# Three-layer graph network: the first two edge steps of layers 1 and 2 gathered before the last two node chunks are stored

## The chip, the core and the metric

One of the eight cores of a Trainium2 chip runs the whole program. The metric is device time in microseconds (us) for one execution, as the median of several. Its engines are named as in the profile: PE (TensorE), DVE (VectorE), ACT (ScalarE), POOL (GpSimd) and SP (SyncE, which only issues DMAs here). "SPq" and "ACTq" are DMAs being issued by SP and ACT.

## What is computed

The reference encodes 12,500 nodes of 64 features, runs three message-passing layers over 212,500 edges sorted by destination, and ends with a readout, a residual and a layer norm. Cut to what matters:

```python
h = node_features @ enc_W + enc_b
for l in range(N_LAYERS):
    cat = jnp.concatenate([h[src], h[dst], edge_features], axis=-1)
    m = jax.nn.relu(cat @ msg_W1[l] + msg_b1[l]) @ msg_W2[l] + msg_b2[l]
    agg = jax.ops.segment_sum(m, dst, num_segments=n_nodes)
    h = _gru_cell(agg, h, gru_Wih[l], gru_Whh[l], gru_bih[l], gru_bhh[l])
return jax.nn.relu(h @ ro_W1 + ro_b1) @ ro_W2 + ro_b2
```

An edge reads its source's row of `h`, so a layer's edges can read any node: layer l + 1 needs every row that layer l makes.

## The kernel before, in words

**Tables.** The product of `h` with the source part and with the destination part of `msg_W1` is made once per node, at the end of a layer's node work, and stored in HBM: `p_tab[l]` (sources) and `q_tab[l]` (destinations), 64 floats a row. An edge then needs a row of `p_tab` (a gather by `src`), a row of `q_tab` (sorted, so a window of 48 rows read by a plain DMA and spread with a one-hot product) and its own attributes.

**Steps.** The edges of a layer are cut into 208 steps of 1,024 edges (8 tiles of 128; the last step has 5). For every step:
- POOL issues one indirect DMA per tile (L734), 128 rows of 256 bytes each, into one of 7 slots of `p_src`. In every fourth step (3, 7, 11, ...) the eighth tile is left to SP and ACT, which issue 64 DMAs of one row each (`single_rows`, L441), so POOL issues 7.
- PE makes the edge part (L872) and the destination part (L873) in PSUM (`mix`). DVE adds the edge part to the gathered rows (L1410, `edge_sums`), adds the destination part (L1413, this sets `joined`), applies relu and a mask (L1424, `drop_masked`), folds runs (L1429, `fold`), and PE spreads the folded rows to nodes (L885). DVE adds these to `sums` (L1439, `keep`, sets `kept`).
- POOL may fill a slot again once the step seven before has been joined.

**Chunks.** The nodes are cut into 26 chunks of 468, then one of 144 and one of 192 (`SPANS`, 28 in all). When the steps that reach a chunk are kept, its GRU runs in stages put between the steps (`chunk_stages`, `fast_chunk`): ACT copies its sums (L1072, L1073), PE makes the gates (L929, L930), ACT and DVE the nonlinear part, PE the next layer's two table rows (L937), ACT copies them to `stage` (L1083) and issues the two stores (L1086, L1087), which raise `stored[0]`. The chunk with index 25 is stored while steps 205 and 206 run, index 26 while step 207 runs, and index 27 after step 207, the last (`END_STAGES`).

**The boundary between layers.** `all_stored` makes POOL, SP and ACT wait until all 28 chunks' tables are in HBM. Then SP and ACT load the windows of the first two groups of four steps (L603, L1111), POOL starts the gathers of step 0, and SP starts the single rows of step 3. The order on each engine is written out by hand, unrolled over layers and steps; only semaphores order the engines among each other:

```python
for l in range(LAYERS):
    all_stored(pool, l, FAST_CHUNKS)
    for m in range(STEPS):
        k, r = l * STEPS + m, (l * STEPS + m) % ROW_SLOTS
        if k >= ROW_SLOTS:
            pool.wait_ge(joined, k - ROW_SLOTS + 1)
        for t in range(gathers_of(m)):
```

## Time and profile before

| | |
|---|---|
| median of 3 runs | 6212.81 us (6212.6 to 6212.83) |
| the profiled execution's own time | 6218.49 us |
| its span, first to last instruction | 6216.6 us |
| POOL busy | 4625.3 us (74%), of it L734 4599.4 us in 4830 instructions |
| DVE busy | 3524.2 us (57%) |
| PE busy | 2874.1 us (46%), weight loads 1569.7 us |
| ACT busy | 345.5 us (6%) |
| DMA | 307.50 MB, mean 49 GB/s |
| chain that ended last | POOL 69%, issue 23%, SPq 3%, DVE 2%, DMA 2%, PE 1% |

How to read it: busy time counts compute and the indirect DMAs' descriptor work on POOL; DMA issues of SP and ACT, waits and register work do not count. The last row follows the work that ended last back to what released each piece of it; "issue" is time in which the engine waited for nothing that the profile shows, here the 0.3 us between two indirect DMAs.

### The profile page before, as it was taken

To read this page: it belongs to the slowest core of one execution; us is meant where nothing else is said; L and a number is where in the kernel's file an instruction comes from. 1 tells how busy PE (TensorE), PEld (TensorE's weight loads), DVE (VectorE), ACT (ScalarE), POOL (GpSimd) and SP (SyncE) were. 2 spreads that over 40 slices of the span, in tenths; PEclk is the share of its full clock that TensorE was granted. 3 is DMA by queue.
4 is the path that set the end of the run, shared out by engine and by line. 5 is a ranking of instruction groups with operands and counts; after the bars stand their busy time and mean duration, and the time that the engine had idled before them with its cause. 6 is when DMAs were issued, how large, how long until landed. Compare 5 with 4: busy or idle time off the path is not lost.

```text
span 6216.6 us, 71434 instructions
## 1 busy us (share of the span) xinstructions
PE 2874.1 (46%) x6986; PEld 1569.7 (25%) x6986; DVE 3524.2 (57%) x4596; ACT 345.5 (6%) x542; POOL 4625.3 (74%) x4865
## 2 busy tenths in 40 slices
PE   4444444444444444444444444444444444444444
PEld 3222222222222222222222222222222222222222
DVE  5555555555555555555555555555555555555555
ACT  1000000000000000000000000000000000000001
POOL 6777777777777677777777777767777777777776
PEclk6666666666656655656555565556566565656656
DMA  4222222222222122222222222212222222222221
GB/s 127 50 49 49 49 49 49 49 49 49 49 49 49 40 48 48 48 48 48 47 48 48 48 48 48 48 44 47 48 48 47 46 49 45 48 48 48 48 48 36
DMA packets 350333, 307.50 MB, mean 49 GB/s; under 512 B 148483, under 2 KB 236553, under 8 KB 349463
## 3 DMA queue, kind: packets, MB, share of 16 engines
q0 software_dynamic: 155328, 159.81, 13.6%
q1 hardware_dynamic: 117167, 109.08, 6.1%
q10 hardware_dynamic: 77328, 33.96, 2.1%
q14 instruction: 453, 3.71, 0.2%
q8 instruction: 57, 0.93, 0.1%
HBM read 279.43 MB, written 22.83 MB: 49 GB/s over the span
## 4 chain that ended last, share of the span: by engine, by line
POOL 69%; issue 23%; SPq 3%; DVE 2%; DMA 2%; PE 1%; ACT 0%; DVEq 0%; ACTq 0%; POOLq 0%
POOL p_src L734 69%; SPq L441 2%; SPq L437 1%; DMA q_tab<-p_src 1%; DVE work_ps L1413 1%; DMA p_src<-p_tab,idx_all 0%; DMA p_src<-p_tab 0%; DVE p_src L1410 0%; PE bank L929 0%; PE bank L930 0%; DVE folds L1429 0%; PE bank L765 0%; DVE state L1448 0%; ACT p_src L994 0%; PE bank L885 0%
## 5 line engine op out<-in xcount | busy, mean ns | idle before, releaser
L734 POOL DMA_INDIRECT p_src<-p_tab,idx_all x4830 | 4599.4, 952 | 1559.0 <-issue 1471.1
L1410 DVE TENSOR_TENSOR p_src<-work_ps,p_src 128x512 f32<-128x512 f32 x624 | 431.2, 691 | 2495.6 <-DMA p_src<-p_tab,idx_all 2283.5
L885 PE MATMUL bank<-hot,folds 128*128 128x96 f32 x2496 | 657.1, 411 | 1855.2 <-DVE folds L1429 1787.9
L872 PE MATMUL work_ps<-w_edges,msg 128*128 128x512 f32 x1248 | 1115.9, 994 | 28.3 <-DMA windows_sb<-q_tab 28.3
L885 PEld LDWEIGHTS bank<-hot,folds 128*128 128x128 f32 x2496 | 528.3, 294 | 2124.6 <-DVE folds L1429 1996.6
L1424 DVE SCALAR_TENSOR_TENSOR work_ps<-work_ps,rel 128x1024 f32<-128x1024 f32 x624 | 768.5, 1232 | 21.5
L1413 DVE TENSOR_TENSOR work_ps<-p_src,bank 128x1024 f32<-128x1024 f32 x624 | 766.8, 1229 | 21.2
L1429 DVE TENSOR_REDUCE folds<-work_ps 128x256 f32<-128x1024 f32 x624 | 757.6, 1214 | 0.1
L882 PE MATMUL bank<-hot,counts 128*34 128x96 bf16 x416 | 66.9, 254 | 909.7 <-DVE folds L1429 909.7
L929 PE MATMUL bank<-state,gate_w 128*128 128x468 f32 x324 | 266.8, 923 | 454.5 <-ACT chunk_sum L1073 324.5
L872 PEld LDWEIGHTS work_ps<-w_edges,msg 128*128 128x128 f32 x1248 | 309.5, 303 | 29.6 <-issue 15.8
L873 PE MATMUL bank<-pick 97*128 97x256 f32 x624 | 313.4, 604 | 0.0
L882 PEld LDWEIGHTS bank<-hot,counts 128*34 128x34 bf16 x416 | 26.6, 106 | 1027.0 <-DVE folds L1429 1006.1
L873 PEld LDWEIGHTS bank<-pick 97*128 97x128 f32 x624 | 204.9, 328 | 312.4 <-issue 312.4
L873 PE MATMUL bank<-windows_sb,pick 97*128 97x256 f32 x624 | 281.0, 546 | 0.0
L873 PEld LDWEIGHTS bank<-windows_sb,pick 97*128 97x128 f32 x624 | 181.1, 290 | 265.2 <-issue 265.2
L929 PEld LDWEIGHTS bank<-state,gate_w 128*128 128x128 f32 x324 | 93.2, 319 | 589.7 <-issue 428.6
L930 PE MATMUL bank<-chunk_sum,sum_w 128*128 128x468 f32 x324 | 225.5, 791 | 0.0
L1072 ACT COPY chunk_sum<-sums 64x468 f32<-64x468 f32 (+1 forms) x84 | 47.3, 563 | 3123.2 <-DVE sums L1439 3118.2
L1439 DVE TENSOR_TENSOR sums<-bank,sums 128x96 f32 x624 | 156.5, 251 | 5.6 <-PE bank L885 2.7
L1383 DVE TENSOR_TENSOR hot<-rel_first,bank 128x784 f32<-128x784 f32 x156 | 149.7, 959 | 0.0
L930 PEld LDWEIGHTS bank<-chunk_sum,sum_w 128*128 128x128 f32 x324 | 96.5, 300 | 123.2 <-issue 123.2
(157 smaller groups left out, 1428.1 us busy)
## 6 DMA issues: line engine op xcount, KB each, us to landing
p_src<-p_tab ACTq DMA_DIRECT2D x9792, 0.2 KB
p_src<-p_tab SPq DMA_DIRECT2D x9792, 0.2 KB
p_src<-p_tab,idx_all POOLq DMA_INDIRECT x4830
msg<-in_edge_k SPq DMA_DIRECT2D x156, 256.0 KB
pick<-rel_tab SPq DMA_DIRECT2D x312, 96.0 KB
windows_sb<-q_tab ACTq DMA_DIRECT2D x312, 24.0 KB
windows_sb<-q_tab SPq DMA_DIRECT2D x312, 24.0 KB
pick<-q_tab ACTq DMA_DIRECT2D x312, 24.0 KB
```

What stands on the lines that cost most here:

```text
L734: pool.indirect_dma_start(out=p_src[r][0:rows, t, :], out_offset=None, in_=p_tab[l][0:NODES, :], in_offset=bass.IndirectOffsetOnAxis(ap=id ...
L872: nc.tensor.matmul(edge_ps[k % 2], attrs[n % 2][:, s, :], w1_edges[:, l, :], start=True, stop=True)
L873: nc.tensor.matmul(node_ps[k % 2], hot_rows[n % 2][0:ROWS + 1, s * 128:(s + 1) * 128], windows_of[k % (2 * GROUP)][0:ROWS + 1, :], start=T ...
L885: last = nc.tensor.matmul(fold_ps, folds[:, b, :], hot_all[n % 2][:, s * BLOCKS + b, 1:WINDOW + 1], start=(b == 0), stop=(b == BLOCKS - 1))
L929: nc.tensor.matmul(ps[:, 0:w], gate_w[:, l, g:g + 128], state[:, here], start=True, stop=False)
L930: end = nc.tensor.matmul(ps[:, 0:w], sum_w[:, l, g:g + 128], chunk_sum[:, 0:w], start=False, stop=True)
L1383: nc.vector.tensor_tensor(hot_all[n % 2][:], first, spots_ps.unsqueeze(1).to_broadcast([128, GROUP * BLOCKS, HOT]), ALU.is_equal)
L1410: nc.vector.tensor_tensor(rows, edge_ps[k % 2], rows, ALU.add).then_inc(with_edge, 1)
L1413: nc.vector.tensor_tensor(both_ps[k % 2].rearrange("p (f b j g) -> p b j g f", b=BLOCKS, j=2, g=RUN), rows.rearrange("p (b g f) -> p b g f ...
L1424: nc.vector.scalar_tensor_tensor(runs, runs, 0.0, edge_masks, ALU.max, ALU.mult).then_inc(masked, 1)
L1429: nc.vector.tensor_reduce(folds[:].rearrange("p b (j f) -> p (b j) f", j=2), both_ps[k % 2].rearrange("p (f e g) -> p e f g", g=RUN, f=HID ...
L1439: nc.vector.tensor_tensor(sums[:, here], fold_ps, sums[:, here], ALU.add).then_inc(kept, 1)
```

## The change

Two constants say what is early: `EARLY = 2` steps of layers 1 and 2, and `LATE = 26 * 468 = 12168`, the first node of the last two chunks. The "late" rows are the 336 from 12168 to 12504, in three blocks of 112.

- **POOL**, in layers 1 and 2, first waits only for the first 26 chunks' stores and for two cleared slots. It gathers steps 0 and 1 from `p_tab[l][0:LATE]` with a bounds check that skips a row beyond it (`oob_is_err=False`). Only ahead of step 2 does it wait for all stores.
- **DVE** clears those two slots at step 204 of the layer before (two memsets of 128 x 512).
- **SP** loads the late rows of `p_tab` into SBUF (one DMA of 112 x 3 x 64) between the window loads of groups 0 and 1 of layers 1 and 2. In layer 0 it also loads the sources of steps 0 and 1, repeated over 112 partitions (two DMAs of 112 x 1024).
- **DVE** compares these sources with the late nodes' numbers (`make_late`): 12 one-hot tiles of 112 x 256 for each early step, in a ring of four buffers. Each tile after the fourth waits for PE.
- **PE** multiplies them by the late rows (24 matmuls of 112 x 128 by 112 x 64 for each early step) into a PSUM bank, ahead of that step's `mix`.
- **DVE** adds the bank to the slot (`add_late`, one 128 x 512 add) ahead of `edge_sums`.
- Four tiles of the final layer norm become slices of one (`normed`) that also holds the one-hot ring. Three small DVE operations at the start make the late nodes' numbers.

```diff
+            if l:
+                pool.wait_ge(stored[0], 32 * (FAST_CHUNKS * (l - 1) + CHUNKS - 1 + ENC_PAIRS // 2))
+                pool.wait_ge(slots_clear, EARLY * l)
             for m in range(STEPS):
                 k, r = l * STEPS + m, (l * STEPS + m) % ROW_SLOTS
                 if k >= ROW_SLOTS:
                     pool.wait_ge(joined, k - ROW_SLOTS + 1)
+                if early(l, m):
+                    for t in range(gathers_of(m)):
+                        pool.indirect_dma_start(
+                            out=p_src[r][:, t, :], out_offset=None, in_=p_tab[l][0:LATE, :],
+                            in_offset=bass.IndirectOffsetOnAxis(ap=idx_all[:, m, t:t + 1], axis=0),
+                            bounds_check=LATE - 1, oob_is_err=False).then_inc(gathered[r], 16)
+                    continue
+                if m == (EARLY if l else 0):
+                    all_stored(pool, l, FAST_CHUNKS)
...
                         group_windows(l, n0 + g, g)
...
+                        if l and g == 0:
+                            sp.dma_start(late_rows, p_tab[l][LATE:NLAST, :].rearrange("(b p) f -> p b f", p=LATE_ROWS)).then_inc(late_in, 16)
+                    if l == 0:
+                        sp.wait_ge(prepared, 8)
+                        for m in range(EARLY):
+                            sp.dma_start(src_seen[m], io["src_early"][m:m + 1, :].to_broadcast([LATE_ROWS, STEP])).then_inc(early_in, 16)
...
+                if early(l, m):
+                    pe.wait_ge(late_in, 16 * l)
+                    for q in range(4):
+                        hots = nth_late(l, m, q, 0)
+                        pe.wait_ge(late_ready, hots + LATE_BLOCKS)
+                        for t in range(2):
+                            at = (2 * q + t) * HID
+                            for b in range(LATE_BLOCKS):
+                                last = nc.tensor.matmul(late_ps[m][:, at:at + HID], late_hot[(hots + b) % 4][:, t * 128:(t + 1) * 128], late_rows[:, b, :],
+                                                        start=(b == 0), stop=(b == LATE_BLOCKS - 1))
+                        last.then_inc(late_mixed, LATE_BLOCKS)
...
+            def make_late(l, m):
+                for q in range(4):
+                    for b in range(LATE_BLOCKS):
+                        i = nth_late(l, m, q, b)
+                        if i >= 4:
+                            dve.wait_ge(late_mixed, (i - 4) // LATE_BLOCKS * LATE_BLOCKS + LATE_BLOCKS)
+                        nc.vector.tensor_tensor(late_hot[i % 4], src_seen[m][:, q * QUARTER:(q + 1) * QUARTER], late_node[:, b:b + 1].to_broadcast([LATE_ROWS, QUARTER]),
+                                                ALU.is_equal).then_inc(late_ready, 1)
+            def add_late(l, m):
+                k = l * STEPS + m
+                rows = p_src[k % ROW_SLOTS].rearrange("p t f -> p (t f)")
+                dve.wait_ge(gathered[k % ROW_SLOTS], landed(k))
+                dve.wait_ge(late_mixed, nth_late(l, m, 0, 0) + LATE_HOTS)
+                nc.vector.tensor_tensor(rows, late_ps[m], rows, ALU.add).then_inc(late_added, 1)
+                dve.wait_ge(late_added, (l - 1) * EARLY + m + 1)
...
+                        if l and m == 0:
+                            dve.wait_ge(early_in, 16 * EARLY)
+                            make_late(l, 0)
+                        if early(l, m):
+                            add_late(l, m)
                         edge_sums(k)
                         drop_masked(k)
+                        if early(l, m + 1):
+                            make_late(l, m + 1)
+                        if m == STEPS - 4 and l < LAYERS - 1:
+                            for j in range(EARLY):
+                                nc.vector.memset(p_src[(k + 4 + j) % ROW_SLOTS], 0.0).then_inc(slots_clear, 1)
```

The order of instructions, engine by engine, shows where these land. POOL's whole gather order, in the kernel before:

```order
L724 COMPARE_AND_BRANCH
L734 DMA p_src<-p_tab,idx_all 128x64 x1609
L734 DMA p_src<-p_tab,idx_all 20x64
L734 DMA p_src<-p_tab,idx_all 128x64 x1609
L734 DMA p_src<-p_tab,idx_all 20x64
L734 DMA p_src<-p_tab,idx_all 128x64 x1609
L734 DMA p_src<-p_tab,idx_all 20x64
L724 UNCONDITIONAL_BRANCH
```

And in the changed one:

```order
L755 COMPARE_AND_BRANCH
L776 DMA p_src<-p_tab,idx_all 128x64 x1609
L776 DMA p_src<-p_tab,idx_all 20x64
L767 DMA p_src<-p_tab,idx_all 128x64 x16
L776 DMA p_src<-p_tab,idx_all 128x64 x1593
L776 DMA p_src<-p_tab,idx_all 20x64
L767 DMA p_src<-p_tab,idx_all 128x64 x16
L776 DMA p_src<-p_tab,idx_all 128x64 x1593
L776 DMA p_src<-p_tab,idx_all 20x64
L755 UNCONDITIONAL_BRANCH
```

The count and order of gathers is the same; 16 in each of layers 1 and 2 (L767) have moved ahead of the wait for all stores, which now stands between them and the 1593.

PE at the start of layer 1, from the last chunk's table product (`w_nodes`) on, in the kernel before:

```order
L937 MATMUL bank<-w_nodes,state 96x128 x2
L872 MATMUL work_ps<-w_edges,msg 128x512
L873 MATMUL bank<-windows_sb,pick 128x256
L872 MATMUL work_ps<-w_edges,msg 128x512
L873 MATMUL bank<-windows_sb,pick 128x256
L885 MATMUL bank<-hot,folds 128x96 x2
```

And in the changed one, where `dst_i` is the memory that holds the late rows and `normed` the one-hot ring:

```order
L990 MATMUL bank<-w_nodes,state 96x128 x2
L922 MATMUL bank<-dst_i,normed 128x64 x24
L925 MATMUL work_ps<-w_edges,msg 128x512
L926 MATMUL bank<-windows_sb,pick 128x256
L922 MATMUL bank<-dst_i,normed 128x64 x24
L925 MATMUL work_ps<-w_edges,msg 128x512
L926 MATMUL bank<-windows_sb,pick 128x256
L938 MATMUL bank<-hot,folds 128x96 x2
```

Each of the first two steps' products now stands behind 24 small ones, and the second 24 stand ahead of the first step's spreading (L938).

DVE at the same place, from the last chunk's new state on, in the changed kernel (before, L1464 is followed at once by L1410, L1413, L1424, L1429 of step 0):

```order
L1536 TENSOR_TENSOR state<-bank,zdiff 64x192
L1478 TENSOR_TENSOR normed<-dst_i,late_node 112x256 x12
L1487 TENSOR_TENSOR p_src<-bank,p_src 128x512
L1463 TENSOR_TENSOR p_src<-work_ps,p_src 128x512
L1466 TENSOR_TENSOR work_ps<-p_src,bank 128x16x64
L1496 SCALAR_TENSOR_TENSOR work_ps<-work_ps,rel 128x1024
L1478 TENSOR_TENSOR normed<-pre,late_node 112x256 x12
L1501 TENSOR_REDUCE folds<-work_ps 128x256
L520 TENSOR_LOAD base_i
L1487 TENSOR_TENSOR p_src<-bank,p_src 128x512
L1463 TENSOR_TENSOR p_src<-work_ps,p_src 128x512
L1466 TENSOR_TENSOR work_ps<-p_src,bank 128x16x64
```

The second step's twelve one-hot tiles stand between the first step's mask (L1496) and its fold (L1501).

## Rows read from the trace of the kernel before

**Rows 1.** The page's busy times, and what its engines waited for: POOL.
```profile
PE 2874.1 (46%) x6986; PEld 1569.7 (25%) x6986; DVE 3524.2 (57%) x4596; ACT 345.5 (6%) x542; POOL 4625.3 (74%) x4865
POOL p_src L734 <- issue: 1471.1, 4817, 0.3
POOL p_src L734 <- DMA q_tab<-stage: 47.2, 2, 27.9
POOL p_src L734 <- DMA q_tab<-p_src: 37.7, 1, 37.7
```
**Rows 2.** Timeline of POOL between layers 0 and 1 (start, us, engine, line, [idle before]).
```profile
2088.18 0.92 POOL L734 DMA_INDIRECT p_src<-p_tab,idx_all  x1 [0.30 <-issue]
2116.98 0.98 POOL L734 DMA_INDIRECT p_src<-p_tab,idx_all  x1 [27.89 <-DMA q_tab<-stage]
...
2137.13 0.95 POOL L734 DMA_INDIRECT p_src<-p_tab,idx_all  x1 [0.31 <-issue]
```
**Rows 3.** The same between layers 1 and 2.
```profile
4140.43 0.90 POOL L734 DMA_INDIRECT p_src<-p_tab,idx_all  x1 [0.30 <-issue]
4160.66 0.98 POOL L734 DMA_INDIRECT p_src<-p_tab,idx_all  x1 [19.33 <-DMA q_tab<-stage]
```
**Rows 4.** Timeline between layers 0 and 1, the other engines: last stores, first step.
```profile
2085.27 0.40 ACTq L1087 DMA_DIRECT2D q_tab<-stage  x1
2114.76 0.44 ACTq L1087 DMA_DIRECT2D q_tab<-stage  x1
2121.49 2.05 PE L872 MATMUL work_ps<-w_edges,msg 128*128 128x512 f32 x2 [7.53 <-DMA windows_sb<-q_tab]
2122.47 24.93 SPq L441 DMA_DIRECT2D p_src<-p_tab  x64
2123.33 1.06 PE L873 MATMUL bank<-windows_sb,pick 97*128 97x256 f32 x2
2128.77 0.69 DVE L1410 TENSOR_TENSOR p_src<-work_ps,p_src 128x512 f32<-128x512 f32 x1 [16.02 <-DMA p_src<-p_tab,idx_all]
2129.49 1.23 DVE L1413 TENSOR_TENSOR work_ps<-p_src,bank 128x1024 f32<-128x1024 f32 x1
```
**Rows 5.** Timeline between layers 1 and 2, around steps 204 and 206.
```profile
4119.58 0.25 DVE L1439 TENSOR_TENSOR sums<-bank,sums 128x96 f32 x1
4119.86 0.58 ACT L1072 COPY chunk_sum<-sums 64x468 f32<-64x468 f32 x1 [17.37 <-DVE sums L1439]
4136.83 0.69 DVE L1410 TENSOR_TENSOR p_src<-work_ps,p_src 128x512 f32<-128x512 f32 x1 [0.16 <-DMA p_src<-p_tab,idx_all]
```
**Rows 6.** Groups by form (busy us, mean ns of one): nearest to the added operations.
```profile
L1499 DVE MEMSET pick<- 128x512 f32 x2 | 1.0, 485 | 0.1
L1478 DVE TENSOR_TENSOR ysq<-yc 117x256 f32<-117x256 f32 x26 | 11.0, 425 | 0.9
L1505 DVE TENSOR_TENSOR rel_first<-dst_i,base_all 128x416 f32<-128x416 int32 x1 | 0.8, 754 | 0.0
L781 PE MATMUL bank<-w_nodes,enc_b_last 64*97 64x64 f32 x4 | 0.9, 380 | 1.1 <-ACT count_w L1002 1.1
```
**Rows 7.** Timeline: spreading matmuls, first at the lower and then at the higher clock.
```profile
2133.30 1.17 PE L885 MATMUL bank<-hot,folds 128*128 128x96 f32 x4 [7.37 <-DVE folds L1429]
2053.54 0.69 PE L885 MATMUL bank<-hot,folds 128*128 128x96 f32 x4
```
**Rows 8.** Timeline in layer 2: gathers beside a DVE operation with two SBUF inputs.
```profile
6150.32 0.95 POOL L734 DMA_INDIRECT p_src<-p_tab,idx_all  x1 [0.30 <-issue]
6150.55 0.42 DVE L1478 TENSOR_TENSOR ysq<-yc 117x256 f32<-117x256 f32 x1
6151.58 0.95 POOL L734 DMA_INDIRECT p_src<-p_tab,idx_all  x1 [0.30 <-issue]
```
**Rows 9.** What SP's queue waited for (us in total, times, longest).
```profile
SPq L591 <- PE bank L873: 906.5, 103, 35.7
SPq L610 <- DVE sums L1439: 400.8, 28, 17.0
```

More of the change, by code:

```diff
@@ L54 @@
 GATHER_SLOTS = LOOP_STEPS
+EARLY = 2
+LATE = (CHUNKS - 1) * CHUNK
+LATE_BLOCKS = 3
+LATE_ROWS = (NLAST - LATE) // LATE_BLOCKS
+QUARTER = STEP // 4
+LATE_HOTS = 4 * LATE_BLOCKS
 LAST_EDGES = EDGES - (STEPS - 1) * STEP
@@ L135, in build @@
         masks = rel[:].rearrange("p s t -> p (s t)").bitcast(BF16).rearrange("p (b j g) -> p b j g", j=2, g=RUN)
+        dst_flat = dst_i[0:LATE_ROWS].rearrange("p s t -> p (s t)")
+        late_rows = dst_flat[:, STEP:STEP + LATE_BLOCKS * HID].bitcast(F32).rearrange("p (b f) -> p b f", f=HID)
+        late_node = sb("late_node", [LATE_ROWS, LATE_BLOCKS])
         rel_first = sb("rel_first", [128, STEPS, BLOCKS])
@@ L179, in build @@
         offsets = p_src[ROW_SLOTS].rearrange("p t f -> p (t f)")[0:GROUPS, 0:128].bitcast(I32)
+        src_seen = [dst_flat[:, 0:STEP], both[0:LATE_ROWS, :].bitcast(I32)]
         first_i = both[0:STEPS // 2, 0:2 * BLOCKS * 128].bitcast(I32)
@@ L202, in build @@
         x_rows = sb("x_rows", [CPART, 4, HID])
-        y = sb("y", [CPART, 4, HID])
-        yc = sb("yc", [CPART, 4, HID])
-        ysq = sb("ysq", [CPART, 4, HID])
+        normed = sb("normed", [CPART, 4, 4, HID])
+        y, yc, ysq, y_out = (normed[:, s] for s in range(4))
+        late_hot = [normed[0:LATE_ROWS, s].rearrange("p j f -> p (j f)") for s in range(4)]
         ysum = sb("ysum", [CPART, 4])
@@ L211, in build @@
         rstd = sb("rstd", [CPART, 4])
-        y_out = sb("y_out", [CPART, 4, HID])
         bank = [ctx.enter_context(nc.psum_tensor(f"bank{i}", [128, 512], F32)) for i in range(5)]
@@ L292, in build @@
         act_singles = [sem(f"act_singles{s}") for s in range(SINGLE_SEMS)]
+        early_in = sem("early_in")
+        slots_clear = sem("slots_clear")
+        late_in = sem("late_in")
+        late_ready = sem("late_ready")
+        late_mixed = sem("late_mixed")
+        late_added = sem("late_added")
         hot_t_ready = sem("hot_t_ready")
@@ L419, in run_slow, with early, nth_late @@
                     chunk_stage(l, j, LOOPED, last)
+        def early(l, m):
+            return l > 0 and m < EARLY
+        def nth_late(l, m, q, b):
+            return ((l - 1) * EARLY + m) * LATE_HOTS + q * LATE_BLOCKS + b
+        late_ps = [zr_ps[:], n_ps[:]]
         def gathers_of(m):
@@ L726, in _ @@
                 for l in range(LAYERS):
-                    all_stored(pool, l, FAST_CHUNKS)
+                    if l:
+                        pool.wait_ge(stored[0], 32 * (FAST_CHUNKS * (l - 1) + CHUNKS - 1 + ENC_PAIRS // 2))
+                        pool.wait_ge(slots_clear, EARLY * l)
                     for m in range(STEPS):
@@ L1508, in _ @@
                 nc.vector.tensor_copy(row_ps, row_f[:]).then_inc(in_psum, 1)
-                dve.wait_ge(in_psum, 2)
+                for b in range(LATE_BLOCKS):
+                    nc.vector.tensor_scalar(late_node[:, b:b + 1], row_i[0:LATE_ROWS, :], 1.0, float(LATE + LATE_ROWS * b), ALU.mult, ALU.add).then_inc(in_psum, 1)
+                dve.wait_ge(in_psum, 2 + LATE_BLOCKS)
                 make_hot(0)
@@ L1588 @@
         "src_single": src[GROUP - 1::GROUP, BLOCKS - 1, :, RUN - 1],
+        "src_early": src[0:EARLY].transpose(0, 1, 3, 2).reshape(EARLY, STEP),
         "dst": dst[place].transpose(2, 0, 1, 3).reshape(128, STEPS, EDGE_TILES),
@@ L1612 @@
         arrays[name] = v = np.ascontiguousarray(v)
-        dt = U32 if name == "src" else I32 if name.startswith("dst") or name == "src_single" else F32
+        dt = U32 if name == "src" else I32 if name.startswith("dst") or name.startswith("src_") else F32
         if name == "src":
```

## The prediction

> **What bounds the kernel now.** I read the busy times and POOL's waits first. POOL is busy for 74% of the span, DVE for 57%, PE for 46% [rows 1]. POOL's idle time is nearly all accounted for in three rows: 1471.1 us in 4817 gaps of at most 0.3 us between two gathers, which is part of issuing one, 37.7 us before the first gather, and 47.2 us in two waits for `q_tab` stores. So POOL never pauses inside a layer. One gather takes 0.95 + 0.30 us; over the 16 from 2116.98 to 2137.13 that is 1.26 us each [rows 2]. 4830 of them, with the three waits and the tail, are the kernel. DVE and PE are waited for only at the layers' ends.
>
> Next, the timeline at both boundaries. Between layers 0 and 1 the last gather starts at 2088.18 and the next at 2116.98: 27.89 us idle [rows 2]. Between layers 1 and 2 it is 19.33 us [rows 3]. In both, what ends the wait is the last chunk's `q_tab` store, issued at 2114.76 and landed when POOL starts 2.22 us later [rows 2, 4]. Call that moment T, the time at which all tables are stored. Only POOL's idle time ahead of T can be won, so the most that this change can give is 27.9 + 19.3 = 47.2 us, less what early work doesn't fill.
>
> **The change, part by part.**
>
> *The 16 moved gathers.* 16 at 1.26 us are 20.15 us. At the first boundary POOL would go on at 2089.4, end its 16 at 2109.6, and wait 7.4 us for T at 2116.98. Step 2 then starts at 2117.0 in place of 2137.13: 20.1 us won, if T stays. At the second, the next gather would have started near 4141.6; 16 later is 4161.75, after T (4160.66). Before, step 2 started 16 gathers after 4160.66, at 4180.8. That is 19.0 us won, with POOL never idle.
>
> *May they start that early?* They wait for chunk 25's stores. At the first boundary its `q_tab` store is issued at 2085.27 [rows 4]; with the 2.22 us that the last store took, it has landed at 2087.5, 1.9 us ahead of POOL's need. The slots are cleared and joined some twenty us earlier.
>
> *The two memsets at step 204*, 128 x 512 each: 0.485 us by the like form [rows 6], with gaps 1.0 us of DVE ahead of the `keep` that releases chunk 25. At the first boundary DVE soon after stands 0.95 us idle for PE, so I take 0.1 us (0 to 1.0). At the second, `keep` at 4119.58 releases ACT at 4119.86 directly, and DVE follows with hardly a gap until step 206, which stood 0.16 us for its gather [rows 5]: T moves by 1.0 - 0.16 = 0.84 us, to 4161.5. POOL arrives at 4161.75 anyway, so it costs nothing there (bounds 0 and 0.8 us, if POOL comes first).
>
> *The skipping bounds check* has no row. Every gather here is of the plain kind, at 1.26 us [rows 2]. Below: nothing, since the skipped rows (336 of 12504 nodes, 3 or 4 of 128 rows) might even save packets, but POOL's own part is fixed. Above I have only DVE's row for an operation with an extra input, which says nothing of POOL; I bound it by another 0.95 us, doing a gather's work twice. I take nothing, as 125 of the 128 rows take the plain path. The first boundary hides 7.4 us, that is 0.46 us a gather; the second hides none.
>
> *The late rows' products.* They lie behind T, on PE and DVE, and POOL feels them only through a slot: step 8 refills step 1's. After T POOL issues the gathers of steps 2 to 7, 46 of them (8 + 7 + 8 + 8 + 8 + 7), which is 57.9 us. So step 1 must be joined by T + 57.9.
> - Start: PE began step 0 at 2121.49, T + 4.5 [rows 4]; one more SP DMA stands between the windows, so T + 5.
> - A matmul: 112 x 128 weights and 64 columns. The nearest row is L781, 97 columns of weights and 64 moving, 0.91 us for two (four passes), 0.46 each; the other side is L885, 128 weights and 96 moving, 1.17 us for two, 0.59 each [rows 6, 7]. I take 0.5, so 3.0 us for the six of a quarter (2.7 to 3.5 at the lower clock; 2.1 at the higher, by the 0.69 us row).
> - A one-hot tile: 112 x 256 with two SBUF inputs, by L1478 0.425 us plus a gap, 0.46; above, L1505's int32 form at 0.754 [rows 6].
> - The ring of four holds one tile more than a quarter. So after the first quarter DVE makes two tiles while PE waits, then PE runs six matmuls while DVE waits: 0.9 + 3.0 + 0.3 for the hand-overs = 4.2 us a round. A step is 3.0 + 3 x 4.2 = 15.6 us.
> - Step 0: products until T + 20.6, edge and destination parts (2121.49 to 2124.39) 2.9, the two adds 2.0 [rows 4]: joined at T + 25.5. The mask 1.3, three tiles 1.4, products 15.6, parts 2.9, adds 2.0: step 1 joined at T + 48.7.
>
> That is 9 us ahead of POOL's need, so I put the products at zero. With 3.5 us and 0.754 us a round is 5.4 us and step 1 is joined at T + 57.8, still free. Behind it DVE needs some 5.5 us a step and POOL 9.7, so the lag of DVE is gone by about step 7, and step 9 (POOL at T + 68) needs step 2, at about T + 56.
>
> *SP.* Its single rows of step 3 took 24.93 us [rows 4] and end near T + 34, before DVE comes to step 3. Group 2's inputs wait for `mixed` of step 3, now near T + 55, then step 7's 64 rows end near T + 85. POOL needs step 7 joined for step 14, at T + 117. SP stood idle 906.5 us for PE in 103 waits [rows 9], so it catches up within a few groups.
>
> *Start and end.* In layer 0 two more DMAs and three tiny DVE operations stand ahead of nothing that POOL waits for; the final chain only changes the addresses of four tiles. Nothing.
>
> **Sum.** 20.1 - 0.1 + 19.0 = 39.0 us. Against the profiled execution: 6218.5 - 39.0 = 6179.5. That execution stands 5.7 us above the median of the runs; against the median, 6212.8 - 39.0 = **6173.8 us**, 0.63% faster. About 0.2%, 12.4 us, is what a measurement of this kernel can tell from no change.
>
> **A rule weighed.** Twelve of a step's tiles have two SBUF inputs and run while POOL gathers. In layer 2 such an operation (0.42 us at 6150.55) lies across two gathers of 0.95 us that start 1.26 us apart [rows 8], the same as everywhere; it cost POOL nothing. The Trainium skill, page "SBUF — State Buffer", section "SBUF: two separate sides", says that DVE and GpSimd share a port pair, taken for a whole instruction by a DVE operation with two SBUF inputs against a GpSimd operation that reads SBUF, and that the other is blocked. The trace does not agree for these gathers; the rule's time is the third rival.
>
> **Rivals.**
> 1. *The products come too late, and a new wait on `joined` replaces the old one.* For it: DVE and PE take turns, nothing like this ring has a row, and waits add up over six rounds. Against it: 9 us of room. It costs from 5.7 us a round on. At 9 us it eats the whole gain (six rounds by 4.8 more are 28.8, less 9.1 of room, 19.7 a boundary). At 11 us a round, 6.8 more in each of six, the stall is 31.7 us a boundary, and the kernel is slower by 63.4 - 39.0 = 24.4 us: 6237. A milder form, 8 us a round, stalls 13.7 a boundary: 6201.
> 2. *The skipping gathers cost more.* Nothing speaks for it but the missing row. At 0.95 us more a gather the 16 take 15.2 us more: 15.2 - 7.4 = 7.8 at the first boundary and 15.2 at the second, so 23 of 39 us are lost: 6197.
> 3. *The one-hot tiles hold POOL back.* If each of the 48 delays a gather by its own 0.425 us, that is 20.4 us: 6194. Against it, rows 8.
> 4. *It doesn't start early.* Chunk 25's stores land later beside the extra traffic, or a slot is not free, and POOL waits about as long as before: the 1.9 us of margin at the first boundary is thin, though beyond it a delay costs only its own length. All of the gain lost: 6213.
>
> **Chances.** The forecast 0.83; the products 0.03 in the strong form and 0.02 in the mild; the gathers 0.05; the tiles 0.03; not early 0.04. Faster by over 0.2% (below 6200.4): forecast, gathers and tiles, 0.91. Within 0.2%: the mild products and not early, with some of what else could be wrong, 0.06. Slower: 0.03. The forecast's own range is 6171 to 6182: from 2 us under the sum (39.5 us with no memset cost, and a like shift of the program's other parts) to both memsets counted in full and stores that land a few us later beside POOL's gathers. I reach to 6190 for a price of the skip of up to half a us and for part of rival 3: **6171 to 6190**.
>
> **What would show it.** POOL's idle before the first early gather 0.3 us at both boundaries; before step 2, about 7.5 us and 0.3 us; the early gathers 0.95 us each; no POOL wait on L1466 (`joined`) behind it; step 1's L1466 done by T + 49, with PE and DVE taking turns every 4.2 us. Wrong: early gathers longer than 1.4 us, a POOL wait at step 7, 8 or 9, or T more than 1 us later after POOL's last gather than before.

## The result, and the profile after

| | before | changed |
|---|---|---|
| median of the runs of one chip, us | 6212.82 (6212.6 to 6213.8, 4 runs) | 6175.56 (6174.51 to 6177.06, 4 runs) |
| ratio, 95% interval | | 0.9939 [0.9926, 0.9953] |
| profiled execution, us | 6218.49 | 6174.51 |
| its span, us | 6216.6 | 6172.7 |

The forecast was 6173.8 us, in a range of 6171 to 6190. The time came 1.8 us above it; the medians differ by 37.3 us, and the forecast said 39.0. The two profiled executions differ by 43.9 us of span, more than the medians, because the one of before stands 5.7 us above its median and the one of the changed kernel 1.05 below.

First the busy times of the changed kernel's page, and what POOL waited for (us in total, times, longest us), which answer to [rows 1].

```profile
PE 2896.9 (47%) x7178; PEld 1598.8 (26%) x7178; DVE 3544.3 (57%) x4655; ACT 345.5 (6%) x542; POOL 4626.0 (75%) x4865
POOL p_src L776 <- issue: 1466.0, 4785, 5.2
POOL p_src L776 <- DMA q_tab<-p_src: 35.2, 1, 35.2
POOL p_src L767 <- issue: 9.7, 32, 0.3
POOL p_src L776 <- DVE work_ps L1466: 3.7, 12, 0.3
```

The two waits of 47.2 us for `q_tab<-stage` are gone from the list. PE does 192 matmul records more and DVE 59 operations more, and neither shows up among what POOL waits for: its longest wait for DVE's join (L1466) is 0.3 us, the ordinary gap.

Now POOL's timeline at the first boundary (start, us, engine, line, [idle before]), the answer to [rows 2].

```profile
2084.60 0.91 POOL L776 DMA_INDIRECT p_src<-p_tab,idx_all  x1 [0.31 <-issue]
2085.82 1.06 POOL L767 DMA_INDIRECT p_src<-p_tab,idx_all  x1 [0.30 <-issue]
...
2105.50 1.00 POOL L767 DMA_INDIRECT p_src<-p_tab,idx_all  x1 [0.30 <-issue]
2111.68 0.96 POOL L776 DMA_INDIRECT p_src<-p_tab,idx_all  x1 [5.18 <-issue]
```

And at the second, for [rows 3].

```profile
4115.11 0.90 POOL L776 DMA_INDIRECT p_src<-p_tab,idx_all  x1 [0.30 <-issue]
4116.32 1.05 POOL L767 DMA_INDIRECT p_src<-p_tab,idx_all  x1 [0.30 <-issue]
...
4136.13 1.00 POOL L767 DMA_INDIRECT p_src<-p_tab,idx_all  x1 [0.30 <-issue]
4137.58 0.96 POOL L776 DMA_INDIRECT p_src<-p_tab,idx_all  x1 [0.45 <-issue]
```

POOL goes from its last plain gather to the first early one without a stop, issues 16 of them 1.31 us apart, and waits 5.18 us for T at the first boundary and 0.45 at the second. (The profile puts these waits down to "issue"; they end within 0.4 us of the start of SP's windows, which wait for the same stores, at 2111.31 and 4137.18, so I read them as waits for T.)

Last, DVE and PE with POOL in between, in the first step's products, and the joins of steps 0 and 1 (L1487 adds the late rows, L1466 joins). A matmul leaves two records in these rows, so x12 is a quarter's six.

```profile
2116.16 2.79 PE L922 MATMUL bank<-dst_i,normed 112*128 112x64 f32 x12 [7.96 <-DMA windows_sb<-q_tab]
2118.99 1.09 DVE L1478 TENSOR_TENSOR normed<-dst_i,late_node 112x256 f32<-112x256 int32 x3 [10.54 <-PE bank L922]
2119.81 2.82 PE L922 MATMUL bank<-dst_i,normed 112*128 112x64 f32 x12 [0.85 <-DVE normed L1478]
2122.66 1.10 DVE L1478 TENSOR_TENSOR normed<-dst_i,late_node 112x256 f32<-112x256 int32 x3 [2.58 <-PE bank L922]
2123.06 1.19 POOL L776 DMA_INDIRECT p_src<-p_tab,idx_all  x1 [0.30 <-issue]
2123.48 2.82 PE L922 MATMUL bank<-dst_i,normed 112*128 112x64 f32 x12 [0.85 <-DVE normed L1478]
...
2133.39 1.23 DVE L1466 TENSOR_TENSOR work_ps<-p_src,bank 128x1024 f32<-128x1024 f32 x1
2150.97 0.69 DVE L1487 TENSOR_TENSOR p_src<-bank,p_src 128x512 f32<-128x512 f32 x1 [1.85 <-PE bank L922]
2154.39 1.23 DVE L1466 TENSOR_TENSOR work_ps<-p_src,bank 128x1024 f32<-128x1024 f32 x1
```

The turns of PE and DVE are plain to see: 2116.16, 2119.81, 2123.48, one every 3.67 us. Step 0 is joined at 2134.62, T + 23.3, and step 1 at 2155.62, T + 44.3 (T here is the start of SP's windows, 2111.31; counted from POOL's own start after T, 0.37 us later, they are 22.9 and 43.9). POOL issues step 8's first gather, which needs step 1's slot, at 2170.48, after the ordinary 0.30 us. And one thing that is new: the gather at 2123.06, beside three one-hot tiles, took 1.19 us where its neighbours take 0.95.

### The profile page after: what moved, and what is told of

Read it like the earlier page. It is cut to its first block, busy times and chain, and to the rows that moved or that the text cites. A ratio compares the mean times of both kernels' runs of the same rounds, so it can differ in the third digit from the quotient of the medians.

```text
span 6172.7 us, 71924 instructions
## 1 busy us (share of the span) xinstructions
PE 2896.9 (47%) x7178; PEld 1598.8 (26%) x7178; DVE 3544.3 (57%) x4655; ACT 345.5 (6%) x542; POOL 4626.0 (75%) x4865
## 3 DMA queue, kind: packets, MB, share of 16 engines
q0 software_dynamic: 155328, 159.79, 13.6%
## 4 chain that ended last, share of the span: by engine, by line
POOL 68%; issue 23%; SPq 3%; DVE 2%; PE 2%; DMA 1%; ACT 0%; ACTq 0%; DVEq 0%; POOLq 0%
POOL p_src L776 68%; SPq L466 2%; PE bank L922 1%; DVE work_ps L1466 1%; SPq L462 1%; DMA q_tab<-p_src 1%; DMA p_src<-p_tab,idx_all 0%; DVE p_src L1463 0%; DMA p_src<-p_tab 0%; DVE folds L1501 0%; PE bank L982 0%; DVE normed L1478 0%; PE bank L983 0%; PE work_ps L925 0%; ACT p_src L1047 0%
## 5 line engine op out<-in xcount | busy, mean ns | idle before, releaser
L938 PE MATMUL bank<-hot,folds 128*128 128x96 f32 x2496 | 650.1, 408 | 1792.0 <-DVE folds L1501 1757.0
L938 PEld LDWEIGHTS bank<-hot,folds 128*128 128x128 f32 x2496 | 523.0, 291 | 2057.7 <-DVE folds L1501 1965.0
L1496 DVE SCALAR_TENSOR_TENSOR work_ps<-work_ps,rel 128x1024 f32<-128x1024 f32 x624 | 768.5, 1232 | 21.6
L1466 DVE TENSOR_TENSOR work_ps<-p_src,bank 128x1024 f32<-128x1024 f32 x624 | 766.9, 1229 | 21.3
L1501 DVE TENSOR_REDUCE folds<-work_ps 128x256 f32<-128x1024 f32 x624 | 757.7, 1214 | 0.0
L925 PEld LDWEIGHTS work_ps<-w_edges,msg 128*128 128x128 f32 x1248 | 306.3, 301 | 13.6 <-DMA windows_sb<-q_tab 13.5
L935 PEld LDWEIGHTS bank<-hot,counts 128*34 128x34 bf16 x416 | 26.6, 106 | 1029.1 <-DVE folds L1501 1008.6
```

The costliest lines, as they stand in the source:

```text
L925: nc.tensor.matmul(edge_ps[k % 2], attrs[n % 2][:, s, :], w1_edges[:, l, :], start=True, stop=True)
L938: last = nc.tensor.matmul(fold_ps, folds[:, b, :], hot_all[n % 2][:, s * BLOCKS + b, 1:WINDOW + 1], start=(b == 0), stop=(b == BLOCKS - 1))
L1466: nc.vector.tensor_tensor(both_ps[k % 2].rearrange("p (f b j g) -> p b j g f", b=BLOCKS, j=2, g=RUN), rows.rearrange("p (b g f) -> p b g f ...
L1496: nc.vector.scalar_tensor_tensor(runs, runs, 0.0, edge_masks, ALU.max, ALU.mult).then_inc(masked, 1)
L1501: nc.vector.tensor_reduce(folds[:].rearrange("p b (j f) -> p (b j) f", j=2), both_ps[k % 2].rearrange("p (f e g) -> p e f g", g=RUN, f=HID ...
```

## Where the 37 us come from

The time from the start of the last plain gather of a layer to the start of step 2's first gather of the next, in the two profiled executions: 48.95 us before (from 2088.18, 16 gathers after 2116.98) and 27.08 after, so 21.9 us less; at the second boundary 40.37 (4140.43 to 4180.80) and 22.47, so 17.9 less. That is 39.8 us together. The other 4.1 us of the difference of the spans lie where nothing was changed: the first gather starts 2.5 us earlier, layer 0's gathers take 1.1 us less, layer 2's and the tail 0.7 less, layer 1's 0.1 more.

The two boundaries differ from the forecast in opposite directions: 1.9 us more at the first, where T came 1.7 sooner, and 1.1 less at the second, where the longer form of the early gathers took 0.8. The distance from the start of the last plain gather to T (here the start of SP's windows) isn't the same in every execution. In the kernels of this study that ran on chips of the first kind (below), it was 28.9 us at the first boundary before, and 26.7, 25.2, 24.2, 26.6 and 29.1 us in five executions with early gathers. At the second boundary it was 20.3 before and 22.1, 22.5, 21.2, 23.0 and 21.2 in the five. One more execution has the kernel before's order (skip_form_3, below): 26.8 and 19.3. So the first one scatters over 5 us with no order that I can name, and the kernel before's order alone moves it by 2.1 us; the second is 0.9 to 3.8 us later in every kernel with early gathers than in either execution without them.

## Experiments

The changed kernel's own account leaves five things to be tested: whether the gain is the filled idle time and nothing else; whether the products are free, and because of the room that I worked out; whether the early gathers are long because of their form; whether the one-hot tiles make gathers long; and what other chips say. Chips turned out to be of two kinds: on two of them the kernel before took 6210 and 6211 us, on two others 9775 and 9789. Each run is compared with the kernel before on its own chip.

**The changed kernel again.** No edit.

> The changed kernel again, beside the kernel before, as the ground of the other runs of this set. Every theory expects 6175.6 us within 1.5, a ratio of 0.994.

Measured 6174.76 us (6172.93 to 6175.59) against 6211.24, ratio 0.9943 [0.993, 0.9957]. The gain of 36.5 us stands.

**One early step in each layer.**

```diff
-EARLY = 2
+EARLY = 1
```

> One early step in each layer in place of two. My theory is that the gain is POOL's idle time ahead of the moment T at which all tables are stored, filled by early gathers one for one. Eight gathers of 1.3 us fill 10.5 us, POOL waits at each boundary for T, about 16 us at the first (5.2 + 10.5) and 9 to 11 at the second, and what is won is about 10 us a boundary instead of 20: the kernel takes 6193 to 6196 us. Rival, that part of the gain comes from elsewhere (another order of the stores, or T that comes earlier by itself once fewer rows are loaded): more than half of the 37 to 44 us stays, 6190 or less. Rival, that a second step of products costs POOL something: then the loss is below 18 us for the same reason, 6191 or less, with POOL's idle still 10.5 us more at each boundary.

Measured 6193.39 us (6189.47 to 6197.05, 10 runs), ratio 0.9973 [0.9964, 0.9982]: 18.6 us slower than two early steps. Its POOL timeline, the first gather after T at each boundary:

```profile
2110.54 0.96 POOL L776 DMA_INDIRECT p_src<-p_tab,idx_all  x1 [13.12 <-issue]
...
4144.34 0.96 POOL L776 DMA_INDIRECT p_src<-p_tab,idx_all  x1 [10.13 <-issue]
```

POOL's waits for T are 23.3 us together, where the changed kernel of the same set has 3.69 + 0.77 = 4.5 us: 18.8 us more idle, 18.6 us more time. The gain is filled idle time, one for one. Both rivals, 6190 or less and 6191 or less, lie below the measured median. 13.1 us at the first boundary is less than the 16 that I wrote, because T came early in this execution (24.2 us after the last plain gather's start).

**No products.** The tiles, the matmuls and L1487 are left out, so the late rows are missing from four steps.

```diff
-                if early(l, m):
+                if False:
                     pe.wait_ge(late_in, 16 * l)
...
-                            make_late(l, 0)
...
                         if early(l, m):
-                            add_late(l, m)
+                            pass
...
-                        if early(l, m + 1):
-                            make_late(l, m + 1)
```

> The early gathers stay, the one-hot tiles, their matmuls and the adding of the late rows are left out, so the late nodes' rows are missing from two steps of layers 1 and 2. My theory, that the products lie in the 58 us that POOL has after T before it needs a slot, expects the changed kernel's time within 2 us, 6174 to 6177. Rival, that tiles with two SBUF inputs hold POOL: a gather beside a run of them took 1.17 to 1.20 us in place of 0.95, at up to 8 places a boundary, so this kernel is 2 to 4 us faster, 6172, and the long gathers are gone. Rival, that the late join of the first steps costs POOL somewhere later in the layer: more than 4 us faster.

Measured 6174.87 us (6171.86 to 6175.34), against 6174.76 for the changed kernel beside it: no difference. 96 matmuls, 48 tiles and four adds cost nothing that these runs can see; their scatter of 3.5 us may hide 1 or 2 us. In its trace no gather from 2118 to 2150 is longer than 0.96 us; the changed kernel has four of 1.17 to 1.20 in that place, and each of the four lies beside one-hot tiles. With the three of 1.10 to 1.19 at the second boundary they are about 1.5 us longer in all. That it was the tiles, and not the matmuls or the adds that are left out with them, this run alone doesn't show; the runs of tiles below do.

**Every product twice.** The second pass writes the same result.

```diff
-                        for t in range(2):
+                        for t in (0, 1, 0, 1):
```

> Every matmul of the late rows is issued twice (24 more a step, 0.46 us each); the result is the same. My theory puts step 1 joined 44.3 us after T in the changed kernel, and POOL's need of its slot at T + 58 (46 gathers): 13.6 us of room. A round grows by 2.8 us and both steps by 22.5, so step 1 is joined at T + 66.5 and POOL waits 8 to 9 us for L1466 before step 8, at each boundary, with perhaps more at step 9: 6191 to 6196 us. Rival, that the slack is not where I put it, because SP or ACT with its single rows sets when the first steps are joined: no or little change if they hold it anyway (below 6180), and a stall at steps 9 to 14 rather than at 8. Rival, that matmuls overlap with DVE's tiles better than turns allow: step 1 by T + 58 and no stall, 6176.

Measured 6189.93 us (6186.88 to 6191.09), ratio 0.9966 [0.9952, 0.9979], 15.2 us above the changed kernel. POOL's timeline before step 8 at the two boundaries, and the join that releases it at the first:

```profile
2181.03 0.95 POOL L776 DMA_INDIRECT p_src<-p_tab,idx_all  x1 [7.04 <-DVE work_ps L1466]
...
4211.10 0.95 POOL L776 DMA_INDIRECT p_src<-p_tab,idx_all  x1 [6.20 <-DVE work_ps L1466]
```
```profile
2179.53 1.23 DVE L1466 TENSOR_TENSOR work_ps<-p_src,bank 128x1024 f32<-128x1024 f32 x1
```

The stall is where the prediction put it, at step 8 and on L1466, and nowhere else. With step 2 at 2116.23, POOL needed the slot at 2181.03 - 7.04 = 2173.99, 57.8 us later; the forecast's count of 46 gathers gave 57.9. Step 1 was joined at 2180.76, 64.5 us after POOL's start behind T, where the changed kernel has 43.9. I had written T + 66.5, a stall of 8 to 9 us and 6191 to 6196 us: the extra 24 matmuls of a step took about 0.43 us each, not 0.46, and the median lies 1 us below that range. Two stalls of 7.04 and 6.20 us, less the ordinary 0.3 of each, make 12.6 of the 15.2 us; the other 2.6 I can't place, and these runs scatter by 4 us. So the products are free because of the slots' room, about 13.6 us in the changed kernel, and what exceeds it was paid here.

**The skipping form on all gathers of the kernel before.** No row is skipped.

```diff
-    in_offset=bass.IndirectOffsetOnAxis(ap=idx_all[0:rows, m, t:t + 1], axis=0)).then_inc(gathered[r], 16)
+    in_offset=bass.IndirectOffsetOnAxis(ap=idx_all[0:rows, m, t:t + 1], axis=0),
+    bounds_check=NODES - 1, oob_is_err=False).then_inc(gathered[r], 16)
```

> The kernel before with the skipping bounds check on all 4830 of its gathers, with the bound at the last node, so that no row is skipped. The early gathers of the changed kernel took 1.00 us and not 0.95, 1.31 us apart and not 1.26. If the form costs this, each gather takes 1.00 us and the kernel 4830 x 0.05 = 240 us more, 6450. If it is the rows that are skipped, or the work beside the early gathers, gathers take 0.95 us and the time is 6213 within 5 us.

Measured 9909.46 us against 9774.53 for the kernel before, one run of each: a chip of the other kind. The gathers' median was 1004 ns there.

> The same kernel as in the run skip_form_all, whose chip ran even the kernel before in 9774.5 us with POOL waiting for slots, so that only the length of one gather could be read there: 1004 ns in place of 953. If the form costs 0.05 us on POOL and POOL is the bound, 6450 us. If something else hides it, 6213.

Measured 9926.15 us (one run) against 9788.61, again such a chip. The 135 and 138 us more are less than the 240 that I expected with POOL as the bound, which it isn't there.

> The kernel of skip_form_all once more. On a chip where the kernel before takes about 6213 us POOL is the bound, and 4830 gathers of 1.004 us in place of 0.953 give 6213 + 246 = 6459 us; if anything but the form made the early gathers long, 6213. On a chip where the kernel before takes about 9780 us, some 140 us more than it, as in the two runs before.

Measured 6464.97 us against 6210.31, one run of each, on a chip of the first kind: 254.7 us more, 0.053 us for each of 4830 gathers. The view of the gathers' line of that run (xcount: duration in ns, minimum/median/maximum):

```profile
L734 POOL DMA_INDIRECT p_src<-p_tab,idx_all x4830: 940/1004/1250, 63.2 to 6432.4; - x194
```

The same line of the kernel before has a median of 952, and the early gathers of the changed kernel (L767) 1005. The form costs 52 ns a gather, whether or not a row is skipped, and it adds up on the bound engine as it should.

**Three more tiles a step, with two inputs in SBUF.** The kernel before, in layer 1 only, in memory that is free there.

```diff
                         fold(k)
+                        if l == 1:
+                            for b in range(3):
+                                nc.vector.tensor_tensor((yc, ysq, y_out)[b][0:112].rearrange("p j f -> p (j f)"),
+                                                        dst_i[0:112].rearrange("p s t -> p (s t)")[:, 256 * b:256 * (b + 1)],
+                                                        row_f[0:112, :].to_broadcast([112, 256]), ALU.is_equal)
```

> The kernel before with three more tiles of 112 x 256 after the fold of every step of layer 1, compared as the one-hot tiles are, both inputs in SBUF, their results not used. If a DVE operation with two SBUF inputs holds a gather as the long ones in the changed kernel suggest, 0.23 us for a run of tiles, layer 1 grows by 0.23 us a step, about 48 us in all. If each tile blocked POOL for its own 0.42 us, 1.26 us a step, 260 us. By my reading of rows 8, that such an operation costs POOL nothing, 6213 within 5 us, and the long gathers had another cause.

> The same kernel as in the run tiles_sbuf, where in a stretch of layer 1 the gathers beside the tiles took 0.95 us but for 12 of 63 that took 1.10 to 1.71. By these, a run of three tiles delays POOL by about 0.06 us on the average: 13 us over the 208 steps of layer 1, 6225 with POOL as the bound. If the 0.23 us of the long gathers of the changed kernel were what every run costs: 6260. If each tile blocked for its own 0.42 us: 6470.

Measured 9729.73 us against 9774.53 (one run of each), and 9744.80 against 9788.61. Both chips were of the other kind, where POOL waits for slots and a longer gather need not cost anything, so the total times say nothing of the question; only the gathers' lengths do. (Why kernels with more work should come out faster there, by 11 to 71 us in these two and the next two, isn't explained.) The timeline of one run of tiles of the first of these:

```profile
5571.95 0.95 POOL L734 DMA_INDIRECT p_src<-p_tab,idx_all  x1 [0.30 <-issue]
5573.17 0.41 DVE L1530 TENSOR_TENSOR yc<-dst_i,row_f 112x256 f32<-112x256 int32 x1
5573.20 1.54 POOL L734 DMA_INDIRECT p_src<-p_tab,idx_all  x1 [0.30 <-issue]
5573.50 0.41 DVE L1530 TENSOR_TENSOR ysq<-dst_i,row_f 112x256 f32<-112x256 int32 x1
5573.84 0.41 DVE L1530 TENSOR_TENSOR y_out<-dst_i,row_f 112x256 f32<-112x256 int32 x1
```

And another run of tiles of the same kernel, with two gathers beside it and neither of them longer; the first starts 0.09 us ahead of the first tile:

```profile
5621.47 0.95 POOL L734 DMA_INDIRECT p_src<-p_tab,idx_all  x1 [0.30 <-issue]
5621.56 0.41 DVE L1530 TENSOR_TENSOR yc<-dst_i,row_f 112x256 f32<-112x256 int32 x1
5621.90 0.42 DVE L1530 TENSOR_TENSOR ysq<-dst_i,row_f 112x256 f32<-112x256 int32 x1
5622.23 0.41 DVE L1530 TENSOR_TENSOR y_out<-dst_i,row_f 112x256 f32<-112x256 int32 x1
5622.73 0.95 POOL L734 DMA_INDIRECT p_src<-p_tab,idx_all  x1 [0.30 <-issue]
```

Counted over 203 runs of tiles in layer 1, 27 gathers took 1.09 us or more (24 in the second kernel of this form), up to 1.71, and all long gathers together 9.8 us more than 0.952 each: 0.05 us a run of tiles. In layer 0 of the same kernel, which has no tiles, 2 of 1610 gathers took over 0.995 us, and none over 1.06. Most gathers beside tiles are not held at all.

Which are held depends on the moment, and the moments were not evenly spread. Of the 25 gathers of the two kernels that started in the 0.25 us behind the start of a run's first tile, 22 took 1.18 to 1.56 us and the other three 0.99 to 1.06. Of the 159 that started in the 0.2 us ahead of it 3 were held, and of the 102 that started 0.25 to 0.36 us behind it one. So the small average holds for the moments at which these chips happened to place the gathers. With every moment of a gather's 1.26 us weighted alike, the same gathers give about 0.13 us a run; that is an estimate, and some of its moments have a single gather.

**The same tiles with one input stream.** The second operand is one number for each partition; the edit is shown against the run above.

```diff
-                                nc.vector.tensor_tensor((yc, ysq, y_out)[b]...,
-                                                        row_f[0:112, :].to_broadcast([112, 256]), ALU.is_equal)
+                                nc.vector.tensor_scalar((yc, ysq, y_out)[b]...,
+                                                        row_f[0:112, :], None, ALU.is_equal)
```

> The same three tiles a step of layer 1, with the second operand as one number for each partition, so that DVE reads one stream from SBUF. If two streams are what holds POOL, the gathers are 0.95 us everywhere and the time is 6213 within 5 us. If any DVE operation of this length beside SBUF holds it, the long gathers are as many as with two inputs.

> The same kernel as in the run tiles_one_in, where long gathers took 1.00 to 1.07 us. If a single stream from SBUF delays POOL by 0.1 us at most, and only at one moment of a gather: at most 5 us over layer 1, 6213 to 6218.

Measured 9763.49 us against 9774.53, and 9717.84 against 9788.61: as above, the totals say nothing. The gathers' line in layer 1 with two inputs, and with one:

```profile
L734 POOL DMA_INDIRECT p_src<-p_tab,idx_all x1595: 899/952/1711, 3399.1 to 6471.5; - x200
```
```profile
L734 POOL DMA_INDIRECT p_src<-p_tab,idx_all x1596: 895/952/1312, 3400.1 to 6471.0; - x200
```

With one stream, 2 gathers of 1.09 us or more in place of 27, but 81 of more than 0.995 in place of 34, nearly all of 1.00 to 1.08; together 8.0 us against 9.8. The first theory of that expectation, 0.95 everywhere, is wrong. But the like sums are an accident of the moments: here 102 gathers of the two kernels started 0.08 to 0.14 us behind a run's first tile, where the kernels with two inputs have 3. At that moment one stream gave 0.95 to 1.08 us in 100 gathers and 1.31 in two, and two streams 1.45, 1.48 and 1.49. So at the same moment two streams hold a gather several times as long. With all moments alike, one stream comes to about 0.02 us a run, by the same kind of estimate. The two operations differ in length too, 0.34 us against 0.42 for the same tile, so the runs don't separate the number of streams from the kind of operation. What the whole time would be with POOL as the bound was not measured; for 208 steps with two inputs, 0.05 to 0.13 us a run would make 10 to 27 us, an estimate.

**The changed kernel on a chip of the other kind.** No edit.

> The changed kernel a third time, on the chip of this set. If POOL is the bound there as it is in the profile of the kernel before, a ratio of 0.994. If the chip is one on which the single rows of SP and ACT hold the kernel (before near 9774 us), POOL's idle time ahead of T is no longer the end of anything, the moved gathers win nothing, and the ratio is 1.00 within its scatter.

Measured 9809.02 us (9781.29 to 9825.61, 10 runs) against 9788.61, ratio 1.0019 [1.0006, 1.0032]: the gain is gone. What POOL waited for, and SP's queue issuing the single rows of one step of layer 1:

```profile
POOL p_src L776 <- DVE work_ps L1466: 3466.6, 216, 30.3
POOL p_src L776 <- issue: 1461.6, 4581, 9.7
POOL p_src L767 <- issue: 110.4, 32, 55.4
```
```profile
5049.91 55.68 SPq L466 DMA_DIRECT2D p_src<-p_tab  x64
```

The changed kernel on the first kind of chip, a like row:

```profile
3025.23 24.86 SPq L466 DMA_DIRECT2D p_src<-p_tab  x64
```

Gathers take the same 0.95 us on both kinds of chip. The issuing of single rows doesn't, and not at all times. Two stretches of those 55.68 us (5055 to 5092 and 5094.2 to 5105.6), and the last gather before the second and the first after it:

```profile
5054.79 35.96 SPq L466 DMA_DIRECT2D p_src<-p_tab  x19
5094.11 11.48 SPq L466 DMA_DIRECT2D p_src<-p_tab  x32
```
```profile
5088.99 0.95 POOL L776 DMA_INDIRECT p_src<-p_tab,idx_all  x1 [0.31 <-issue]
5109.20 0.95 POOL L776 DMA_INDIRECT p_src<-p_tab,idx_all  x1 [19.26 <-DVE work_ps L1466]
```

While POOL gathers, with one pause of 3.2 us, 19 rows take 35.96 us, 1.9 each; while it stands idle, 32 rows take 11.48, 0.36 each, as on the other chip. Over the whole trace, gaps of over 4.5 us left out, SP issues rows 2.2 us apart on the average beside running gathers and 0.39 apart with POOL idle (ACT 1.7 and 0.41), and the traces of four other runs on chips of this kind give SP 2.1 to 2.2 and 0.4. On the first kind it is 0.39 beside gathers that never stop. So the issuing of single rows on this kind of chip is slow only where POOL gathers, and the joins wait for them: POOL waits 3466.6 us for joins in 216 gaps, where it has 3.7 us on the first chip. Ahead of the first early gather it waits 55.4 us; starting steps 0 and 1 early only lengthens a wait that POOL has behind them. Why gathers slow the single rows there and not on the first kind is open, and so is what made the changed kernel 0.19% slower rather than equal; no run was made for either.

## Why the prediction was right, step by step

- **The bound.** Right: POOL never pauses inside a layer, and with one early step fewer 18.8 us more idle time ahead of T made 18.6 us more time. It holds on the kind of chip that the profile came from, and the prediction didn't say that this was a condition.
- **May they start that early.** Right: 0.30 us before the first early gather at both boundaries, in every trace of the first kind of chip. Rival 4 is out.
- **The first boundary.** 20.0 us forecast, 21.9 found. The wait that is left was 5.18 us and not 7.4 (7.7 with the ordinary 0.3 that the row counts): the early gathers are longer by 16 x 0.052 = 0.8 us, and T came 1.7 us sooner. That this is the scatter of T and not the change isn't shown, but in one of the five traces T came 0.2 us later than before, and in skip_form_3, with the old order, 2.1 us sooner.
- **The second boundary.** 19.0 forecast, 17.9 found. T moved by more than the 0.84 us that I gave the memsets: 0.9 to 2.7 us in five traces against the one of before, and 1.8 in the changed kernel's. The prediction named a T more than 1 us later as a sign of being wrong, and here the sign came. It cost little, because POOL comes to T 1 us after the old one anyway: POOL's idle time ahead of step 2 was 0.45, 0.77, 1.53 and 0.30 us in the four traces with two early steps, where 0.3 is the ordinary gap. The memsets can be 1.0 us of the delay (L1604, two of 485 ns, as [rows 6] had it). What the rest is, I haven't separated.
- **The skipping form.** The one term that was wrong in size: "I take nothing, as 125 of the 128 rows take the plain path". It costs 0.052 us for each gather, by its form and not by its rows. It lies inside the bounds (0 to 0.95), is hidden at the first boundary and costs 0.8 us at the second.
- **The products.** Right to call them free, and right in where the room ends (T + 57.9). The terms: a matmul 0.465 us for 0.5; a quarter's six 2.8 for 3.0; a round 3.67 for 4.2, as DVE's two tiles cost PE 0.85 us and there was nothing more for the hand-overs; step 0 joined at T + 23.3 for 25.5 and step 1 at T + 44.3 for 48.7. The need at T + 57.9 was met to 0.1 us in the doubled run. Rival 1 was tested by that run: it is real, and decides from about 13.6 us of delay on.
- **SP.** Right: step 7's join ended at 2197.5, T + 86, and POOL's first gather of step 14, which needs it, starts 32 us later.
- **The rule weighed, and rival 3.** The prediction took from the trace of before that an operation with two SBUF inputs costs POOL nothing. The rule of the Trainium skill's page "SBUF — State Buffer", section "SBUF: two separate sides", is that it blocks a GpSimd operation that reads SBUF, for the whole instruction. Both were too strong. [Rows 8] show one such operation with gathers of 0.95 us, and most of those in layer 1 of the run tiles_sbuf do the same; but some are held for 0.15 to 0.76 us, and nearly all that start just behind the first tile of a run. By each tile's own length it would be the 20.4 us of rival 3; measured, by the long gathers of the changed kernel, about 1.5 us. One row was too few to read "never" from it, and the trace of before had another that says so (start, us, engine, line):

```profile
4852.27 0.42 DVE L1478 TENSOR_TENSOR ysq<-yc 117x256 f32<-117x256 f32 x1
4852.37 1.16 POOL L734 DMA_INDIRECT p_src<-p_tab,idx_all  x1 [0.30 <-issue]
```

- **The sum.** 39.0 us, less 0.8 for the form at the second boundary, less about 0.5 for the later T there, less about 1.5 for the held gathers, is 36.2 us. The medians gave 37.3 and 36.5. That the forecast came within 2 us is in part luck: in the profiled pair its two boundaries are off by 1.9 and 1.1 us in opposite directions, and the form, the held gathers and the later T were each put at nothing or too little.

A better version wasn't run. What is left is 5 us at the first boundary. A third early step there would fill it, but by my estimate its products would add some 15 us on PE and DVE ahead of a join that POOL needs about T + 64, and step 2 would be joined at about T + 44 + 21 = T + 65 by the 21.0 us between the two joins above. At most 5 us, under 0.1%, is less than these runs can tell.

## What to carry to other kernels

Where one engine is the bound and stands idle for a known event, work moved ahead of that event is won one for one, up to the idle time. The extra work that this makes on other engines is free as long as it ends before the bound engine needs a buffer of theirs: count the bound engine's instructions until then; here that came out to 0.1 us. A new form of the instruction on the bound engine is never free by argument: price it by putting it on all instances. Where one operation may hold another, compare them at the same moment of overlap; an average over the moments that a run happened to have doesn't carry over. And such a gain belongs to the bound: on the chips where the single rows were the slower part, the same edit gave nothing.

## What was unexpected of the hardware

- The skipping form of an indirect gather costs 52 ns more (1004 against 952), with no row skipped; over 4830 gathers 254.7 us.
- A gather on POOL is sometimes held by DVE work in SBUF, depending on the moment at which it starts: behind the first of three tiles with two SBUF inputs, by 0.2 to 0.6 us in 22 of 25 gathers that started within 0.25 us, and in 3 of 159 that started in the 0.2 us ahead of it. Where the tiles read one stream, most holds were 0.05 to 0.13 us.
- Two of four chips took 9775 and 9789 us for the kernel that takes 6210 to 6213 elsewhere. There SP issued 256-byte transfers about 2.2 us apart while POOL was gathering and 0.39 apart while it was idle; on the others it is 0.39 beside gathers too. The gathers and most of DVE's and PE's operations had the same lengths on both.
- The time from the last plain gather of layer 0 to T lay between 24.2 and 29.1 us in seven executions, of kernels that differ there only in two memsets, the form of the gathers and whether POOL gathers on.
